# Message table split into three bf16 parts in a graph network kernel: 132 rounds of three gathers and eight fetches, a second sort of 412 columns without pacing

## The reference

```python
def _L3_gnn_ref(x, edge_index, edge_type, edge_emb_W, msg_W, msg_b, upd_W, upd_b, ln_g, ln_b):
    src, dst = edge_index[0], edge_index[1]
    m_in = jnp.concatenate([x[src], edge_emb_W[edge_type]], axis=-1)
    m = jax.nn.relu(m_in @ msg_W.T + msg_b)
    agg = jax.ops.segment_sum(m, dst, num_segments=N)
    deg = jax.ops.segment_sum(jnp.ones_like(dst, dtype=x.dtype), dst, num_segments=N)
    out = (agg / jnp.clip(deg, 1.0)[:, None]) @ upd_W.T + upd_b
    h = x + out                      # then layer norm with ln_g, ln_b
```

## Time and profile before

| | |
|---|---|
| time, median of 3 runs | 5814.91 us (5786.38 to 5836.95) |
| span of the profiled execution | 5410.6 us, 73777 instructions |
| time around the span (median less span) | 404.3 us |
| busy share of the span | PE 62%, weight loads 39%, DVE 75%, ScalarE 35%, GpSimd 72% |
| message rounds | about 4666 to 5383 us of the span |

### The profile page before, as it was taken

The page is one execution under the profiler, slowest core; times in us unless marked ns, Lnnn a source line. Parts: engine busy times, 40 slices in busy tenths (PEclk is TensorE's granted clock), DMA queues, the critical chain, the costliest instruction groups (busy, mean ns, idle before and its releaser), DMA issues. The chain is left out here.

```text
span 5410.6 us, 73777 instructions
## 1 busy us (share of the span) xinstructions
PE 3355.5 (62%) x22778; PEld 2088.4 (39%) x22779; DVE 4043.8 (75%) x6650; ACT 1882.8 (35%) x2462; POOL 3916.5 (72%) x2525
## 2 busy tenths in 40 slices
PE   2322222222222666777633577769999999899999
PEld 1322222222220222222333322224444455699998
DVE  5799989898884998999899899981622101677776
ACT  1000000000001446999744599970001110433334
POOL 0388888888888888999888889986056660478775
PEclk6555555555555778999855799989999999999999
DMA  9622222222225994343699534347675677354554
GB/s 408 222 1 1 1 1 1 1 1 1 1 1 144 357 341 116 106 109 91 193 324 320 161 104 109 91 108 273 249 261 192 222 264 258 108 150 145 152 147 113
DMA packets 507289, 790.27 MB, mean 146 GB/s; under 512 B 294189, under 2 KB 389788, under 8 KB 469400
## 3 DMA queue, kind: packets, MB, share of 16 engines
q1 hardware_dynamic: 336886, 750.71, 41.9%
q0 software_dynamic: 164128, 35.36, 8.8%
q10 hardware_dynamic: 6146, 2.68, 0.2%
HBM read 603.67 MB, written 165.59 MB: 142 GB/s over the span
## 5 line engine op out<-in xcount | busy, mean ns | idle before, releaser
L732 POOL DMA_INDIRECT sorted_edges<-record_slot,place_slot x784 | 1654.8, 2111 | 275.1 <-issue 228.4
L711 POOL DMA_INDIRECT edge_weight_and_count<-weight_and_count,target x784 | 1234.8, 1575 | 448.5 <-issue 244.9
L826 PE MATMUL PS<-consts,key_slot 128*128 128x128 f32 x798 | 198.4, 427 | 1025.5 <-DVE target L1630 1021.9
L770 POOL DMA_INDIRECT feature_major<-message_table,copies_then_records x480 | 565.2, 1178 | 363.9 <-DMA message_table<-node_major 217.7
L782 PE MATMUL PS<-tiles,node_major 128*128 128x448 f32 (+1 forms) x2100 | 817.3, 547 | 9.7 <-ACT node_major L1273 9.7
L782 PE MATMUL PS<-tiles 128*64 128x392 f32 (+1 forms) x3200 | 630.5, 515 | 281.9 <-DVE tiles L1825 280.9
L1825 DVE SCALAR_TENSOR_TENSOR tiles<-tiles,copies_then_records 128x1568 f32<-128x1568 f32 (+1 forms) x400 | 698.6, 1782 | 13.3 <-ACT tiles L1390 12.7
L1767 DVE SCALAR_TENSOR_TENSOR feature_major<-tiles,s,feature_major 128x1600 f32<-128x1600 f32 (+3 forms) x384 | 679.5, 1847 | 19.2 <-ACT tiles L1337 18.8
L751 POOL DMA_INDIRECT paired_edges<-copies_then_records,edges x328 | 327.0, 997 | 347.3 <-issue 302.7
L826 PEld LDWEIGHTS PS<-consts,key_slot 128*128 128x128 f32 x798 | 155.0, 223 | 1047.5 <-DVE target L1630 1043.7
L782 PEld LDWEIGHTS PS<-tiles,node_major 128*128 128x128 f32 (+1 forms) x2100 | 399.5, 193 | 387.3 <-issue 372.5
(11 more groups left out here) (376 smaller groups left out, 4916.8 us busy)
## 6 DMA issues: line engine op xcount, KB each, us to landing
tiles<-edge_weight_turned SPq DMA_DIRECT2D x72, 1568.0 KB, 7.9
tiles<-edge_count SPq DMA_DIRECT2D x72, 1568.0 KB, 8.0
tiles<-edge_weight_and_count SPq DMA_DIRECT2D x48, 1600.0 KB, 9.8
edge_weight_and_count<-feature_major SPq DMA_DIRECT2D x48, 1568.0 KB, 39.3
copies_then_records<-edge_count SPq DMA_DIRECT2D x192, 392.0 KB
tiles<-edge_weight_and_count SPq DMA_DIRECT2D x48, 1536.0 KB, 9.1
feature_major<-types_and_sources SPq DMA_DIRECT2D x119, 512.0 KB
edge_weight_turned<-feature_major SPq DMA_DIRECT2D x48, 768.0 KB
```

Of the source, the lines that this page charges most:

```text
L711: nc.gpsimd.indirect_dma_start(out=edge_d, out_offset=bass.IndirectOffsetOnAxis(ap=idx[:, s, a:a + 1], axis=0), in_=pay[:, s, a, :], in_of ...
L732: nc.gpsimd.indirect_dma_start(out=rec_d, out_offset=bass.IndirectOffsetOnAxis(ap=place_slot[:, s, a:a + 1], axis=0), in_=rec_slot[:, s, a ...
L770: nc.gpsimd.indirect_dma_start(out=msg[i % GATHERED][:, a, :], out_offset=None, in_=table_d, in_offset=bass.IndirectOffsetOnAxis(ap=rec[:, ...
```

## The change

The number of rounds becomes 132, each with GA = 3 gathered blocks and the same eight fetched ones. So NA = 396 columns are used as the first sort leaves them, and MC = 412 are sorted again. Their indirect DMAs no longer wait for tiles; they go out in packets of eight, on two semaphores in turn, a packet when the one before on its semaphore has landed. The table is kept in the core as three bf16 parts whose sum is the float32 value (high, middle, low), made by ScalarE copies and DVE subtractions ahead of the rounds. A fetch is now three bf16 matmuls with the same bf16 one-hot, each with its column from a register. In a round the gathered messages of the round before are scattered first, ahead of the first fill; the second fetched half follows after it. `offsets` reads 7, 8 and 4 numbers. ScalarE bends the gathered block between the two fetched ones. The eight DVE operations that fill `offset_at` move ahead of the last normalisation's scaling, and the turnings of types move from tiles 4 to 20 to tiles 8 to 24. Some buffers move, and some semaphores are merged.

```diff
-ROUNDS = 120
-GA, GB2, GH = 4, 8, 4
+ROUNDS = 132
+GA, GB2, GH = 3, 8, 4
 NA, NB = GA * ROUNDS, GB2 * ROUNDS
 MC = NCH - NA
 RW2 = NB + MC
 PAIR = GA + GB2
 RING = 3
 GATHERED = 6
-OFFSETS = 24
+OFFSETS = GA + 4 * GH
...
-        src_hot = [ring(s, PAIR * TP, GB2 * TP).rearrange("p (b n) -> p b n", n=TP) for s in range(RING)]
-        type_hot = [ring(s, (PAIR + GB2) * TP, PAIR * TP // 2)[0:TYPE_ROWS].bitcast(BF16).rearrange("p (b n) -> p b n", n=TP)
+        src_hot = [ring(s, PAIR * TP, GB2 * TP // 2).bitcast(BF16).rearrange("p (b n) -> p b n", n=TP) for s in range(RING)]
+        type_hot = [ring(s, PAIR * TP + GB2 * TP // 2, PAIR * TP // 2)[0:TYPE_ROWS].bitcast(BF16).rearrange("p (b n) -> p b n", n=TP)
...
+        PART = NT * D // 2
+        table_high = tiles[0:TP, 10176 - PART:10176].bitcast(BF16)
+        table_middle = P3[:, NP - PART:NP].bitcast(BF16)
+        table_low = H[:, NP - PART:NP].bitcast(BF16)
+        table_rest = [tiles[0:TP, RING * ring_words:RING * ring_words + 4 * TP], P0[:, NP - 4 * TP:NP]]
...
-            c = 0
-            for n in range(72):
-                pool.wait_ge(S("tile_free"), NT * (n // 24 + 2) + n % 24 + 4)
-                pool.nop(nofuse=True)
-                for _ in range(MC // 72 + (n < MC % 72)):
-                    nc.gpsimd.indirect_dma_start(
-                        out=part_d, out_offset=bass.IndirectOffsetOnAxis(ap=place2_i[:, c:c + 1], axis=0),
-                        in_=rec[:, NA + c, :], in_offset=None, bounds_check=TP * RW2 - 1).then_inc(S(f"records_sorted{c % 2}"), 16)
-                    c += 1
-            for s in range(2):
-                pool.wait_ge(S(f"records_sorted{s}"), 8 * EC + 16 * MC // 2)
+            pair_packets = [[slice(c, min(c + 8, MC)) for c in range(8 * k, MC, 16)] for k in range(2)]
+            for n in range(len(pair_packets[0])):
+                for k in range(2):
+                    if n:
+                        pool.wait_ge(S(f"records_sorted{k}"), 8 * EC + 16 * 8 * n)
+                        pool.nop(nofuse=True)
+                    for c in range(pair_packets[k][n].start, pair_packets[k][n].stop):
+                        nc.gpsimd.indirect_dma_start(
+                            out=part_d, out_offset=bass.IndirectOffsetOnAxis(ap=place2_i[:, c:c + 1], axis=0),
+                            in_=rec[:, NA + c, :], in_offset=None, bounds_check=TP * RW2 - 1).then_inc(S(f"records_sorted{k}"), 16)
+            for k in range(2):
+                pool.wait_ge(S(f"records_sorted{k}"), 8 * EC + 16 * sum(p.stop - p.start for p in pair_packets[k]))
...
-                    if k == 5 and t in (4, 8, 12, 16, 20):
-                        turn_types(t // 4 - 1)
+                    if k == 5 and t in (8, 12, 16, 20, 24):
+                        turn_types(t // 4 - 2)
...
+            pe.wait_ge(S("spare_results_read"), NT + 2 + STAGES)
+            pe.wait_ge(S("middle_made"), CH)
+            pe.wait_ge(S("low_made"), CH)
...
-                first, n = i * OFFSETS + third * 8, 8 if third < 2 else GH
+                first, n = i * OFFSETS + (0, GH + GA, 3 * GH + GA)[third], (GH + GA, 2 * GH, GH)[third]
...
-                    last = nc.tensor.matmul(out_ap, src_hot[u][:, half * GH + c, :], NMf[:, bass.ds(at[c], D)],
-                                            start=False, stop=True, skip_group_check=True)
+                    for part in (table_high, table_middle, table_low):
+                        last = nc.tensor.matmul(out_ap, src_hot[u][:, half * GH + c, :], part[:, bass.ds(at[c], D)],
+                                                start=False, stop=part is table_low, skip_group_check=True)
                 last.then_inc(S("blocks_filled"), 1)
...
-                    scatter(bent[1], before, GA + GH, at[0:4])
+                    pe.wait_ge(S("messages_made"), i * 1)
+                    scatter(msg[g_before], before, 0, at[0:GA])
                 pe.wait_ge(S("blocks_bent"), i * 3 + 1)
-                fill(u, 0, at[4:8])
+                fill(u, 0, at[GA:GA + GH])
                 at = offsets(i, 1)
                 if not first:
-                    pe.wait_ge(S("messages_made"), i * 1)
-                    scatter(msg[g_before], before, 0, at[0:4])
+                    scatter(bent[1], before, GA + GH, at[0:GH])
                 pe.wait_ge(S("blocks_bent"), i * 3 + 2)
-                fill(u, 1, at[4:8])
+                fill(u, 1, at[GH:2 * GH])
                 scatter(bent[0], u, GA, offsets(i, 2)).then_inc(S("scattered"), 1)
...
+            def middle(g):
+
+                act.wait_ge(S("rest_made"), g + 1)
+                n = len(tiles_of(g)) * D
+                A_(table_middle[:, 4 * g * D:4 * g * D + n], table_rest[g % 2][:, 0:n], ACT.Copy).then_inc(S("middle_made"), 1)
+
             for b in range(CH):
                 act.wait_ge(S("msg_x"), b + 1)
                 n, t = rows_of(tiles_of(b).stop - 1), tiles_of(b)
-                A_(NM[0:n, t.start:t.stop, :], bigT[0:n, t.start:t.stop, :], ACT.Copy).then_inc(S("msg_x_copied"), 1)
+                A_(NM[0:n, t.start:t.stop, :], bigT[0:n, t.start:t.stop, :], ACT.Copy).then_inc(S("table_copied"), 1)
+                part = slice(t.start * D, t.stop * D)
+                act.wait_ge(S("table_copied"), 2 * b + 1)
+                A_(table_high[:, part], NMf[:, part], ACT.Copy).then_inc(S("table_copied"), 1)
+                if b:
+                    middle(b - 1)
+            middle(CH - 1)
...
-                if i:
-                    bend_gathered(i - 1)
                 bend_block(i, 0)
+                bend_gathered(i)
                 bend_block(i, 1)
-            bend_gathered(ROUNDS - 1)
...
+            def before_scale():
+
+                row_hots(1)
+                tile_offsets()
+
+            layer_norm(6, H, before_scale)
...
+            def rest_of(g):
+
+                n = len(tiles_of(g)) * D
+                return table_rest[g % 2][:, 0:n], slice(4 * g * D, 4 * g * D + n)
+
+            def low(g):
+
+                rest, at = rest_of(g)
+                dve.wait_ge(S("middle_made"), g + 1)
+                if g == 0:
+                    dve.wait_ge(S("msg_x"), CH)
+                v.tensor_tensor(table_low[:, at], rest, table_middle[:, at], ALU.subtract).then_inc(S("low_made"), 1)
+
+            for g in range(CH):
+                rest, at = rest_of(g)
+                dve.wait_ge(S("table_copied"), 2 * g + 2)
+                if g >= 2:
+                    dve.wait_ge(S("low_made"), g - 1)
+                v.tensor_tensor(rest, NMf[:, at], table_high[:, at], ALU.subtract).then_inc(S("rest_made"), 1)
+                if g:
+                    low(g - 1)
+            low(CH - 1)
```

More of the change, by code:

```diff
@@ L2130, in _, with tile_offsets @@
                 result(CH - 1)
-            layer_norm(6, H, lambda: row_hots(1))
+            def tile_offsets():
+                at = offset_at.rearrange("p (i j) -> p i j", j=OFFSETS)
+                o(v.memset(offset_at[:, 0:OFFSETS].bitcast(F32), 0.0))
+                o(v.memset(offset_at[:, ROUNDS * OFFSETS:].bitcast(F32), 0.0))
+                sources, targets = (part[0:1, :, k].rearrange("p (i j) -> p i j", j=GB2) for k in range(2))
+                for half, first in ((0, GA), (1, 2 * GH + GA)):
+                    o(v.tensor_scalar(at[:, 0:ROUNDS, first:first + GH], sources[:, :, half * GH:(half + 1) * GH], TP * 31, None, ALU.bitwise_and))
+                for half, first, later in ((0, 3 * GH + GA, 0), (1, GH + GA, 1)):
+                    o(v.tensor_scalar(at[:, later:ROUNDS + later, first:first + GH], targets[:, :, half * GH:(half + 1) * GH], 5, TP * 31,
+                                      ALU.logical_shift_right, ALU.bitwise_and))
+                o(v.tensor_copy(at[:, 1:ROUNDS + 1, 0:GA], tile_at[:, 0:NA].rearrange("p (i j) -> p i j", j=GA)))
+                signal("tiles_made")
@@ L2140, in _ @@
-            for half, first in ((0, 4), (1, 12)):
-                o(v.tensor_scalar(at[:, 0:ROUNDS, first:first + GH], sources[:, :, half * GH:(half + 1) * GH], TP * 31, None, ALU.bitwise_and))
-            for half, first, later in ((0, 16, 0), (1, 0, 1)):
-                o(v.tensor_scalar(at[:, later:ROUNDS + later, first:first + GH], targets[:, :, half * GH:(half + 1) * GH], 5, TP * 31,
-                                  ALU.logical_shift_right, ALU.bitwise_and))
-            o(v.tensor_copy(at[:, 1:ROUNDS + 1, 8:8 + GA], tile_at[:, 0:NA].rearrange("p (i j) -> p i j", j=GA)))
```

60 lines of the change are left out of this document (30 added, 30 removed).

## The result

The changed kernel took 6661.75 us (median of four runs, 6653.01 to 6663.41) against 5810.53 us for the kernel before (5786.38 to 5836.95): 1.148 times, 95% interval 1.143 to 1.152. It is slower, as forecast, but by 851 us where 184 were forecast: 672 us past the forecast of 5990 and 602 past the top of the range.

The account below looks back on a forecast made before the run. The prediction took PE's sequencer queue to become the message stage's bound: +168 us there, +7 at the stage's start and +9 in the second sort, +184 on 5815, forecast 5990 us, range 5870 to 6060.

Parts of the forecast that it names:

- 404.3 us lie around it: Whole kernel: profiled span 5410.6 us against a median of 5814.91; the difference was left as it is.
- 0.083 us plus 0.0635 a number: PE's queue, offset loads: time of one load, read from 591, 337 and 586 ns for 8, 4 and 8 numbers.
- The load of seven: PE's queue, after the first half's four scatters: loading seven offsets takes 0.69 us, plus 0.2 of loop counting.
- unpaced, 412 take 532 us ... : 0, at most 4.: Second sort: GpSimd's unpaced scatters take 532 us and end early enough that DVE's wait covers the reload; cost 0, at most 4.
- Rival (c): Second sort: offsets arrive after 4516, PE stops at the turning of types and all after it moves; 6030 us, chance 0.05.
- the 16 of the forecast: Ahead of the message stage: +7 us for table copies at its start and +9 for the wider second sort.
- The sequencer becomes the bound: Message stage: PE's queue needs 6.65 us a round against the array's 4.72; 6.70 x 132 = 884 us, +168.
- Rival (b): Message stage: the array stays the bound, round 4.72 us, stage 623; 5738 us in all, chance 0.15.
- rival (a): Message stage: queue step is per pass, 0.076 us a bf16 part, round 5.86; 5889 us in all, chance 0.12.
- A fill of 12 parts: PE's queue, each of a round's two fills: 12 addressed parts at 0.11 us a step, 1.32 us.
- the load and the scatters between the fills: PE's queue: load of eight, 0.76, and four scatters, 0.44, make 1.20 us and cover ScalarE's work on the first fill.
- the scatters put ahead of the first fill: Message stage: three gathered scatters moved earlier make PE wait earlier for other engines; taken as 0, at most 0.2 us a round.

Follow-up runs that it names:

- The aligned kernel: Changed kernel with each of a round's three offset loads starting at a multiple of four words: 6318.2 us, 1.095 of before; in another group 5705 us, 1.051.
- after: The changed kernel itself, as profiled, against the kernel before: 6661.75 us, 1.148 times.
- the two aligned kernels: Changed kernel with aligned offset loads, its second sort unpaced in one and paced by tiles in the other: 5705 and 5716 us beside 5426, ratios 1.051 and 1.053.

## Why the prediction was wrong

**The reading of the time.** "The median of the runs is 5814.91, so 404.3 us lie around it; I leave them as they are." Nothing lies around a span here but 1.8 us. The trace was of a quicker execution, and every term was sized at its pace. A gap of 7% between a profiled execution and the runs was the sign; a second look at before shows it at once. The loads cost much at either pace: 330 us at the quicker (all loads of before shifted), 290 at the slower. So does the split: 284 us at the slower, and 139 at the quicker for one of its three parts. The burst costs nothing at the quicker pace and 247 to 308 at the slower.

**The offset loads: the term that failed first.** "so 0.083 us plus 0.0635 a number" was fitted to three loads that all started on a multiple of four words. The diff turned OFFSETS from 24 to 19, which was read as a count alone. The load of seven was put at 0.69 with its surroundings; loads measured 1.06 or 1.70, 0.60 or 1.94, and 0.34 or 1.00. The aligned kernel gives the size, 290 us. The could not show it, as all loads there are aligned.

**The second sort: the step that failed second.** "unpaced, 412 take 532 us ... : 0, at most 4." The duration was near (577 us in after, 557 in the aligned kernel at the quicker pace), and the cost was sought in its end alone. Who works beside the burst was not asked: at the slower pace the instructions of PE and SP crawl for as long as it is unbroken, and 247 us (412 columns) to 264 and 308 (328, in before) are lost. Rival (c) had the wrong mechanism, the records arriving late. That one is seen too, at the quicker pace: GpSimd's load of the pairs starts at 4522.7, for records forecast near 4500, and the first turning of types at 4536.4 for 4515.8. Of these 20.6 us 13 were there from the products ahead, and PE loses some 10. There the message stage starts 32 us later for the 16 of the forecast.

**The queue: right in kind, short in size.** "The sequencer becomes the bound" is what eight parts fewer (139 us), no registers (352 us, some of it perhaps the clock) and no split (284 us) show. Rival (b), the array, and rival (a), 0.076 us a part, are out. The round was forecast at 6.70 us, and with aligned loads, as the forecast supposed them, it took 7.37 at the quicker pace. Its walk, from PE's timeline there:

```profile
5304.87 0.23 PE L1166 MATMUL PS<-attention_sum,tiles 96*128 96x128 bf16 x1
...
5305.30 0.22 PE L1166 MATMUL PS<-attention_sum,tiles 96*128 96x128 bf16 x1
...
5306.24 0.40 PE L1188 MATMUL PS<-feature_major,tiles 128*128 x2
5307.29 1.15 PE L1171 MATMUL PS<-tiles,feature_major 128*128 128x128 f32 x8 [0.65 <-issue]
5308.28 0.22 PE L1166 MATMUL PS<-attention_sum,tiles 96*128 96x128 bf16 x1
5308.34 0.22 PE L1188 MATMUL PS<-tiles 128*128 x1
5308.40 0.27 PE L1188 MATMUL PS<-feature_major,tiles 128*128 x2
```

From the load of four to the first fill the forecast sums to 2.81 us, and 2.77 were taken (5302.10 to 5304.86 on the sequencer). A fill of 12 parts was put at 1.32, and from the first part's regop to that of the next load 1.57 were taken (to 5306.44). So the step is 0.13 us and not 0.11, which the forecast had taken though it named 0.115 as its reading and 0.125 as a bound. That is 0.5 of the missing 0.67 us a round; the load and the scatters between the fills, 1.34 for 1.20, are most of the rest. At the quicker pace this closes the account: 0.67 x 132 = 88 us, and the 16 us more ahead of the stage, on top of the forecast's 184 give 288, where the two aligned kernels stand 279 and 290 us above before. At the slower pace the same kernel takes 8.06: ScalarE bends the first fill late. In this round of it the fill ends at 5403.72 and the bend starts 1.50 us later, for 0.04 at the quicker pace:

```profile
5403.37 0.35 PE L1188 MATMUL PS<-feature_major,tiles 128*128 x2
...
5405.22 0.60 ACT L1552 ACTIVATE feature_major<-PS 128x512 f32<-128x512 f32 x1 [3.31 <-PE PS L1188]
```

In most rounds it is 0.7 to 1.5 us, and 0.04 behind the second fill at either pace; PE's queue stands 0.72 us in the median ahead of the second fill, for 0.11. Why ScalarE starts late no run tells. The last rows of the walk also settle the array's price, where the queue had run ahead behind four scatters (eight matmuls): the parts start 0.06 us apart. The Trainium skill (TensorE: Matmul & The Clock Gate, Back-to-back issue gap) gives about 81 ns for a sustained stream of such pairs of weight load and matmul; the measurement decides, and it decides nothing here, as the queue is the slower.

**What was neutral as said.** GpSimd's gathers are hidden, DVE's changes cost nothing in the stage, and the scatters put ahead of the first fill made no wait.

## What to carry to other kernels

Where operands have addresses from registers, count the steps of PE's queue (0.13 us each here) beside the array: replacing one float32 matmul by three bf16 ones cut the array time that bounded the round (PE 95 to 99% busy), but tripled the steps, and the queue, at 7.37 us a round, passed the 5.92 of the float32 fetch. A table that a sequencer reads is laid out so that each load starts on 16 bytes even if that costs padding, and a changed row length is a changed alignment. An engine whose work is "hidden" may still slow its neighbours, so an issue burst is priced by what they do meanwhile, and paced by them if it need not be early. Before terms are read from a trace, its span is set beside the timed runs.

## What the runs showed of the hardware

- A load of numbers into PE's registers takes 0.59 us for eight and 0.33 for four if it starts on 16 bytes, 1.94 and 1.00 if not: 0.24 us for each number. Seven from an aligned place take 1.06, as if four went together and the last three one by one.
- With GpSimd issuing an indirect DMA each 1.29 us without a pause, moves on its queue took 0.70 us for 0.029, SP's register and branch instructions 0.70 for 0.03 to 0.05, and PE started a matmul in 2.8 us for 0.38, in each of the eight traces of an unpaced sort at the slower pace (some 280 to 510 us of each) and not in the one at the quicker, whose burst is as dense. Why is open: no run tells what the instructions wait for, nor what makes the pace.
- The same program ran at 5426 to 5795 us in groups of runs, at 5426 and 5768 under one and the same chip number, and the loss is not even: none in the first 1950 us, 173 in the message stage (710 and 883 us).
- A matmul whose address comes from a register takes a step of 0.129 us on PE's queue as a bf16 fetch part, the same in the traces at either pace, while bf16 parts that wait in the queue start 0.06 us apart.
